# A decoder layer with routed experts: late groups closer together, two scatter sequences per step, two load queues in the tail, fewer idle products

## The reference

```python
x = x + attn(layernorm(x))                 # 16 heads of 8, rotary positions, softmax over 128 keys
x = x + cross_attn(layernorm(x), ctx_1024) # 16 heads of 8, softmax over 77 keys
x = x + ffn(layernorm(x))
# ffn: logits = x @ Wg + bg; top 2 of 8 experts, softmax over the two
#      y_e = gelu(x @ W1[e] + b1[e]) @ W2[e] + b2[e]   (128 -> 512 -> 128), the two chosen ones weighted
#      layernorm(x + y) * gamma + beta
```

## Time and profile before

| | |
|---|---|
| median of 3 runs | 647.62 us (645.97 to 648.56) |
| the profiled execution's own time | 647.97 us |
| its span, first to last instruction | 646.1 us |
| PE busy | 555.5 us, 86% of the span |
| DVE, ACT, POOL busy | 399.4, 336.5, 334.8 us (62%, 52%, 52%) |
| mean granted PE clock | 0.941 of full |

### The profile page before, as it was taken

How to read it: one execution, slowest core, us unless ns; L and a number is a source line. 1 busy time by engine, 2 the same in 40 slices (tenths; PEclk the granted TensorE clock), 3 DMA queues, 4 the chain that set the end, 5 groups by cost and what they waited for, 6 DMA issues and landing times.

```text
span 646.1 us, 22061 instructions
## 1 busy us (share of the span) xinstructions
PE 555.5 (86%) x7748; PEld 410.8 (64%) x7750; DVE 399.4 (62%) x1351; ACT 336.5 (52%) x869; POOL 334.8 (52%) x461
## 2 busy tenths in 40 slices
PE   4548899899999999999899997998877999999791
PEld 1224656556576666566666775677877999999530
DVE  3375778576677767758667564465666555555275
ACT  1113656466576566566666663354644455555243
POOL 4322735353353683773744655447646444444375
PEclk9687999899999999999999997598998899999996
DMA  3440323214158251060210331012213222221292
GB/s 104 140 138 9 89 73 100 67 55 138 31 183 250 65 168 60 15 196 31 77 51 31 111 88 43 14 44 72 80 54 93 67 70 66 54 58 55 68 261 82
DMA packets 74434, 55.73 MB, mean 86 GB/s; under 512 B 9024, under 2 KB 70981, under 8 KB 74338
## 3 DMA queue, kind: packets, MB, share of 16 engines
q1 hardware_dynamic: 69954, 45.92, 25.4%
q0 software_dynamic: 4384, 8.53, 4.0%
HBM read 33.62 MB, written 19.23 MB: 82 GB/s over the span
## 4 chain that ended last, share of the span: by engine, by line
PE 54%; DVE 20%; issue 9%; POOL 6%; ACT 3%; DMA 3%; SPq 2%; DVEq 2%; POOLq 0%; ACTq 0%
DVE nmp L1205 7%; PE AV L775 7%; PE S L949 7%; PE AV L874 5%; PE ST L743 5%; PE W L819 5%; PE SM L800 3%; PE AV L965 3%; PE SM L965 3%; PE ST L749 3%; PE S L711 2%; DVEq L1484 2%; DVE onorm L1216 1%; PE SM L788 1%; POOL routed L1665 1%
## 5 line engine op out<-in xcount | busy, mean ns | idle before, releaser
L1205 DVE TENSOR_REDUCE nmp<-S 128x4 bf16<-128x512 f32 (+1 forms) x256 | 142.2, 578 | 70.1 <-PE S L711 70.1
L1017 ACT ACTIVATE prob<-ST 128x512 f32<-128x512 f32 (+1 forms) x256 | 138.3, 591 | 73.0 <-PE ST L749 72.7
L1131 ACT ACTIVATE va<-S,b1s 128x128 f32<-128x128 f32 x288 | 82.2, 369 | 77.7 <-PE S L949 76.9
L1730 POOL DMA_INDIRECT expert_out<-va,ks x72 | 71.0, 986 | 72.2 <-DVE va L1511 62.9
L743 PE MATMUL ST<-nmt,onesr 32*77 32x128 bf16 (+1 forms) x1024 | 76.5, 224 | 15.8 <-DVE nmp L1205 12.2
L949 PE MATMUL S<-va 128*128 128x128 f32 x576 | 82.0, 287 | 8.8 <-DVE va L1499 8.6
L743 PEld LDWEIGHTS ST<-nmt,onesr 32*77 32x77 bf16 (+1 forms) x1024 | 55.3, 105 | 49.7 <-issue 45.0
L775 PE MATMUL AV<-prob,va 77*32 77x128 f32 (+1 forms) x2048 | 85.5, 286 | 0.0
L949 PEld LDWEIGHTS S<-va 128*128 128x128 f32 x576 | 73.1, 199 | 14.0 <-DVE va L1499 13.7
L1665 POOL DMA_INDIRECT routed<-pay,dest x64 | 66.0, 1031 | 17.8 <-issue 17.2
L874 PE MATMUL AV<-onesr,idb 128*128 128x256 bf16 x435 | 72.5, 285 | 0.0
(11 more groups left out here) (226 smaller groups left out, 1142.0 us busy)
## 6 DMA issues: line engine op xcount, KB each, us to landing
ks<-routed SPq DMA_DIRECT2D x72, 65.0 KB, 1.8
qs<-q_parts SPq DMA_DIRECT2D x32, 128.0 KB
ks<-k_parts SPq DMA_DIRECT2D x32, 128.0 KB, 2.7
q2s<-q_parts SPq DMA_DIRECT2D x32, 128.0 KB
k2s<-k_parts SPq DMA_DIRECT2D x32, 77.0 KB
xin<-x SPq DMA_DIRECT2D x8, 256.0 KB, 3.2
q_parts<-rpart SPq DMA_DIRECT2D x8, 256.0 KB
k_parts<-rpart SPq DMA_DIRECT2D x8, 256.0 KB, 3.4
```

Source lines behind the costliest of these rows:

```text
L1017: act.activation(prob[0:st.keys, j, :], ST[j % 2][0:st.keys, :], ACT.Exp, scale=SCALE).then_inc(s_exp, 1)
L1131: last = act.activation(ht[:, k, q, :], S[k][:, q * P:(q + 1) * P], ACT.Gelu, bias=b1s[:, bass.ds(b + q, 1)])
L1205: V.tensor_reduce(nmp[:, st.at % 2, row_tile(p), 0:NB], S[p % 2][:, 0:NB * st.keys].rearrange("p (b k) -> p b k", b=NB), AX.X, ALU.max, ne ...
L1730: pool.indirect_dma_start(out=expert_out, out_offset=bass.IndirectOffsetOnAxis(ap=xr[:, c % ROUND, D + 1:D + 2].bitcast(U32), axis=0), in_ ...
```

## The change

Five edits: `LATE` goes from 51 to 43, so that group 3 is late as well and POOL normalises at the end of a step from step 43; late groups scatter one sequence (two scatters) per step over four steps, instead of three scatters per step over three; `add_beta` moves from POOL to DVE for groups 3 and 4; in a step with projections the idle products ahead of `values(before, 1)` go away (`idle_at(st, 1)` is 0) and those ahead of `values(st, 0)` stay at 3; in the tail ACT issues two of the sixteen `y2` loads, PE runs 20 idle products ahead of the sums, POOL keeps the gamma product for chunks 1 and 3 alone, and chunk 7 is finished and stored in halves. With the scatters go semaphores for each sequence instead of one count, and two buffers of row numbers (`dest`).

```diff
-LATE = 51
+LATE = 43
...
+BETA = 3
...
-        if g < EARLY:
+        if g < BETA:
             job(last + 5, "beta", g)
...
-                    n = i * TOPK + k
-                    at, place = (chosen + 1 + n // 3, n % 3) if last >= LATE else (chosen + 1 + i, k)
-                    job(at, ("scatter", place), (g, i, k))
+                    job(chosen + 1 + i, ("scatter", k), (g, i, k))
...
-        def scat_count(g):
-
-            return 16 * (GS * TOPK * (g + 1) + 1)
+        def wait_scattered(eng, g, seqs=range(GS)):
+
+            for i in seqs:
+                eng.wait_ge(s_scat[g % 2][i], 16 * TOPK * (g // 2 + 1))
...
+        ON_POOL = (1, 3)
+        LAST = CHUNKS - 1
...
+        FIRST_Y2 = 2
...
-            sp.wait_ge(s_scat, scat_count(EARLY))
+            for g in (EARLY - 1, EARLY):
+                wait_scattered(sp, g)
             sp.wait_ge(s_tab, 1)
...
+                    if not (k and n < FIRST_Y2):
+                        load_y2(sp, n, k)
...
+            for n in range(LAST):
                 sp.wait_ge(s_fin, n + 1)
...
+                store(n * FC, FC)
+            sp.wait_ge(s_fin, LAST + 1)
+            store(LAST * FC, FC // 2)
+            sp.wait_ge(s_fin, LAST + 2)
+            store(LAST * FC + FC // 2, FC // 2)
...
-            def idle_at(st):
-
-                own = [name for j in range(NJ) for name, g in items_at(st, j)]
-                return 3 if st.slot < SEQS or any(name in PROJECTIONS for name in own) else 6
+            def idle_at(st, m):
+
+                own = sum(name in PROJECTIONS for j in range(NJ) for name, g in items_at(st, j))
+                if own == 0:
+                    return 3 if st.slot < SEQS else 6
+                return (3, 0)[m]
...
                 if before:
-                    dense(idle_at(st), AV[:, 2 * L:4 * L])
+                    dense(idle_at(st, 1), AV[:, 2 * L:4 * L])
...
             for n in range(4):
                 tokens_of(n)
+            pe.wait_ge(s_yw, NT)
+            dense(20, W[0][:, :])
...
             expert_turns(act, turn, between)
-
+            for k in range(4):
+                act.wait_ge(s_sc[k], 16 * NT // 4)
+            for n in range(FIRST_Y2):
+                load_y2(act, n, 1)
...
-                if i in (20, 22, 24):
-                    add_beta(EARLY + (i - 20) // 2)
+                if 20 <= i < 30 and i % 2 == 0:
+                    add_beta(BETA + (i - 20) // 2)
...
+            def chunk_out(n):
+                if n < LAST:
+                    part_out(n, n * FC, FC)
+                else:
+                    part_out(n, n * FC, FC // 2)
+                    part_out(n, n * FC + FC // 2, FC // 2)
```

More of the change, by code:

```diff
@@ L317, in decoder_layer @@
         destf = sb("destf", [P, GS, TOPK])
-        dest = sb("dest", [P, GS, TOPK], I32)
+        dest = sb("dest", [P, 2, GS, TOPK], I32)
         w1s = sb("w1s", [P, E * HID])
@@ L431, in decoder_layer @@
         s_hot = sem("s_hot")
-        s_scat = sem("s_scat")
+        s_scat = [[sem(f"s_scat{r}{i}") for i in range(GS)] for r in range(2)]
+        s_filler = sem("s_filler")
         s_out = sem("s_out")
@@ L669, in _ @@
             sp.wait_ge(s_fill, 16 * (E + 1))
-            sp.wait_ge(s_scat, scat_count(NG - 1))
+            for g in (NG - 2, NG - 1):
+                wait_scattered(sp, g)
             sp.wait_ge(s_tab, 2)
@@ L678, in _, with store @@
                 for k in range(TOPK):
-                    r0 = k * NTOK + n * FC * L
-                    sp.dma_start(y2[n][:, k, :].rearrange("p (s d) -> p s d", d=D),
-                                 expert_out[r0:r0 + FC * L, :].rearrange("(s p) d -> p s d", p=P)).then_inc(s_y2[k][n], 16)
-            for n in range(CHUNKS):
-                sp.wait_ge(s_fin, n + 1)
-                sp.dma_start(out_rows[:, n * FC:(n + 1) * FC, :],
-                             x2all[:, n * FC * D:(n + 1) * FC * D].rearrange("p (s d) -> p s d", d=D)).then_inc(s_out, 16)
-            sp.wait_ge(s_out, 16 * CHUNKS)
+                    if not (k and n < FIRST_Y2):
+                        load_y2(sp, n, k)
+            def store(first, seqs):
+                sp.dma_start(out_rows[:, first:first + seqs, :],
+                             x2all[:, first * D:(first + seqs) * D].rearrange("p (s d) -> p s d", d=D)).then_inc(s_out, 16)
+            for n in range(LAST):
+                sp.wait_ge(s_fin, n + 1)
+                store(n * FC, FC)
[3 more added lines that the diff above has]
+            store(LAST * FC + FC // 2, FC // 2)
+            sp.wait_ge(s_out, 16 * (CHUNKS + 1))
         @block.tensor
@@ L1316, in place @@
                 own = pay[:, g % 2, :, :, :]
+                if g >= 2:
+                    wait_scattered(dve, g - 2)
                 dve.wait_ge(s_gexp, g + 1)
@@ L1638, in norm_instance @@
                 else:
-                    if st.i == 0:
-                        g = st.group
-                        if g == 0:
-                            pool.wait_ge(s_none, 4)
-                        if g >= 2:
-                            pool.wait_ge(s_scat, scat_count(g - 2))
+                    g = st.group
+                    if st.at == CROSS_STEP[0]:
+                        pool.wait_ge(s_none, 4)
+                    if g >= 2:
+                        wait_scattered(pool, g - 2, (st.i,))
+                        if st.i == 0:
                             pool.wait_ge(s_keep[g % 2], 16 * (g // 2))
@@ L1699, in step @@
                     add_beta(g)
-                scatters(n, 2)
                 if n >= LATE:
@@ L1754, in _ @@
                     inverse_deviations(n)
-                if n and (n - 1) % 2:
+                if n - 1 in ON_POOL:
                     pool.wait_ge(s_norm, n * FC)
-                    times_gamma(G, n - 1)
+                    times_gamma(G, (n - 1) * FC, FC, s_gam[1])
 ARRAYS = ("x", "ctx_t", "w_self", "b_self", "bp", "w_cross", "b_cross", "bo", "wg", "bg", "w1", "b1", "w2", "b2",
```

45 lines of the change are left out of this document (25 added, 20 removed).

## The result

The changed kernel took **625.42 us** (median of 4 executions, 622.60 to 627.62), the kernel before, run beside it, 648.09 us (4 executions, 645.97 to 648.97). The ratio is 0.965, with a 95% interval of 0.960 to 0.971. Forecast were 623.6 us, in 615 to 635. The profiled execution took 627.59 us, with a span of 625.7.

The account below looks back on a forecast made before the run. PE was taken as the bound, with POOL's queue making one stall and half clock behind it. Terms of 13.3 + 9.2 + 0.4 - 0.4 + 1.9 = 24.4 us off 647.97 gave 623.6 us, range 615 to 635.

Parts of the forecast that it names:

- The stall and the half clock: Attention stage from step 54: PE's 3.5 us wait for POOL and 27 us at half clock vanish, 13.3 us gained.
- prediction's own tests the first: PE's clock: the prediction is wrong if it drops anywhere between step 10 and the first turn.
- the second fails at group 6: Test on PE's waits: the prediction is wrong if POOL is still the one that PE waits for.
- The idle products: Projection steps up to 53: three fewer idle products, 0.33 us at each of 29 groups; 9.2 us gained, bounds 4.8 to 9.6.
- the second rival: At `x3t` of group 6 or the first load: stall stays or returns, one half-clock stretch, 635 us; chance 0.15.
- Group 3 late: Around step 48: `choose` no longer precedes `norm_rows` on DVE; half of a 0.83 us wait saved, 0.4 us.
- Beta: Between turns: two more additions on DVE cost 0.4 us, bounds nothing to 1.4 us.
- The tail: Final sums and stores: 0.6 us lost at the first sum, 2.1 and 0.4 gained at the end; 1.9 us gained.
- The sign of under 4.5 us: Tail: the next profile would show under 4.5 us from L1553's counterpart to the last addition.
- The slower rival: Projection steps: fewer products let the clock fall, 11 us per 27 us stretch, 657 us with three; chance 0.06, 0.04 slower.

Follow-up runs that it names:

- POOL's order alone: Changed kernel with the idle products and tail of the kernel before, against the kernel before: 637.7 us, ratio 0.983.
- tail of before: Changed kernel with the kernel before's tail (one load queue, no 20 idle products, last chunk whole), against the kernel before: 626.6 us, ratio 0.966.
- without the 20: Changed kernel without the 20 idle products of 512 columns ahead of the final sums, against the kernel before: 625.2 us, ratio 0.965.
- sets 1 and 2: Two groups of follow-up kernels, each run on one chip beside the kernel before, which took 650.3 and 649.6 us there.
- three scatters: Changed kernel with late groups' scatters again three, three and two to a step, against the kernel before: 633.7 us, ratio 0.977.
- k2 earlier: Changed kernel with the k2 projection of group 7 one step earlier, against the kernel before: 622.6 us, ratio 0.960.
- set 3: Third group of follow-up kernels, run on one chip beside the kernel before, which took 700.7 us there.

## Why the prediction was right, point by point

- **The stall and the half clock: 13.3 forecast, 13.5 measured.** The mechanism is the one forecast; POOL's order alone shows it. In the changed kernel SP's first load comes 21.86 us earlier, step 54 8.35 us: 13.5. That this agrees to 0.2 us is in part luck, for two misses cancel: counted from step 54, `x3t` of group 6 comes 13.9 us earlier and not 15.3, since the wait for `k2s` stands ahead of it, and the first load loses 0.4 us behind it and not 2.0. SP waited for the scatter there, as forecast: its first load comes 3.5 us behind the start of the last scatter. But that starts 6.2 us behind `x3t` of group 6 where 7.2 were taken, and so the load comes only 1.4 us behind the table (1.1 before). Of the prediction's own tests the first holds from step 11 to the first turn, where the clock is full; a stretch of half clock at 113 to 120 us lies in steps 9 and 10. By the letter the second fails at group 6, where PE still waits 0.83 us for POOL.
- **The idle products: 9.2 forecast.** Each projection step is 0.33 us shorter, but for steps 26 and 34 (0.08) and step 29 (0.8). Steps 1 to 8 and 11 to 53 of the changed kernel with the tail of before are 10.3 us shorter than with POOL's order alone, so the term was 1 us small. Steps 9 and 10 took 1.9 us back in the changed kernel's trace (a wait of 2.85 us for `ks` from `k_parts`, 1.86 before, and 6.8 us at half clock instead of 3.4). The kernel without the 20 has the same 6.8 us there; six other traces of sets 1 and 2 with the idle edit have no half clock in these steps. **What the step missed** is the k2s wait of step 57. I looked for what PE meets later among DVE's waits and not among SP's transfers. It costs 1.3 us and, in some executions, a stretch of half clock: the second rival, with another cause than it named. PE's being faster explains only part of it. The transfer that parks `k2` in `k_parts` and the product that needs `k2s`, before and after:

```profile
380.38 0.37 SPq L559 DMA_DIRECT2D k_parts<-k2part  x1
388.89 0.25 PE L743 MATMUL ST<-nmt,onesr 32*77 32x128 bf16 x2
...
371.85 0.37 SPq L572 DMA_DIRECT2D k_parts<-k2part  x1
```

Before, 8.5 us pass between them without a wait. After, PE is there 8.2 us behind the parking and starts at 381.34, 9.5 us behind it. So PE comes 0.3 us earlier, and the transfers are ready at least 1.0 us later, counted from the parking; in the six other traces with this wait they take 9.1 to 10.3 us. Why they take longer is open.
- **Group 3 late: 0.4 forecast, 0.6 measured**: with POOL's order alone, steps 46 to 50 take 25.65 us instead of 26.22 (step 46 longer by 1.2; 47, 48 and 50 shorter).
- **Beta: -0.4 forecast.** The expert stage lost 1.1 us. That beta is its cause is not borne out: three other kernels with the addition on DVE (POOL's order alone, tail of before, without the 20) took 169.5 to 170.2 us, less than the 170.7 before, so 1.1 us is within what traces differ by. Up to the next load behind the fillers SP's queue carries the time (it starts 63.3 us after the first load before and 63.4 after), and what PE gains between turns ends in the longer wait (4.50 us, 2.69 before). What the last 1.0 us went into is open.
- **The tail: +1.9 forecast, -0.4 measured. This is the term that failed**, in three of its pieces. At the first sum I took 1.0 us of delay by the 20 products and nothing by the second queue: it is 1.2 us, and by the queue, behind which the first load lands 1.2 us later (4.09 us instead of 2.93), while the products end within that wait. What the products give back, full clock behind a wait of over 3 us, I did not count, since the trace of before had it anyway. At the end, L1582 takes 0.17 us as forecast, and gamma and residual of a half chunk 0.43 and 0.42 us where I took 0.36: from L1582 to the last addition pass 5.5 us instead of 7.2, so -1.7 of -2.1. (The sign of under 4.5 us did not follow from the sum, which gives 5.1.) What was not in the sum at all is the end of the path. I followed DVE's last addition and the store, but before and after the span ends with POOL's closing piece; SP was through 2.5 us behind the last addition before and 2.0 after, so the store did get shorter and never counted. POOL's last instruction comes 2.4 us earlier (+31.6 instead of +34.0), and the closing piece, by the split semaphores, is 2.8 us longer: together the 0.4 us lost.
- **The slower rival** (the clock falls in projection steps): not seen between steps 11 and 53 of the changed kernel. Of the eight traces of sets 1 and 2 and the result that have the idle edit, two have one stretch of half clock of 3.4 us there: three scatters in step 41 (1.5 us longer) and k2 earlier in step 24 (0.8 us longer); the two without the edit have none. So the rival may be at work at a small price, which no run here settles. Half clock beside the wait for `k2s` is the larger risk.

In all, 24.4 us were forecast and 22.7 came between the medians (20.4 between the profiled spans). The executions of the changed kernel come in two kinds, 623 and 627.6 us (granted clock 0.96 and 0.95), and the profiled one is of the longer kind.

## What to carry to other kernels

When work is taken from the engine that leads, list the transfers whose start it sets and whose end it waits for: they do not get faster with it (here they took longer), and the first of them to be late is the next stall. Two edits that each take time from the same clock-bound stretch are to be run apart and together; here one alone could cost most of its own gain. A block of transfers on an in-order queue costs what stands behind it, and spreading it among the loads was worth about a third of the whole change (5.9 to 6.5 us between the first load and the last scatter, 8 to 9 us in the medians). And the end of a program has a price of its own: read what lies between each engine's last instruction and the end of the span.

## What the hardware showed unexpected

- Half clock held for 64.8 us with PE busy 63.2 of 64.7 us: a busy PE is no guarantee that the clock returns soon. It held for 20 to 27 us in four other stretches of the traces outside set 3.
- A wait of 1.21 us was followed by half clock, one of 1.30 us in nearly the same code was not.
- POOL's closing piece takes 4.5 us with one semaphore for its scatters and the filler, 7.3 with nine, 7.1 with five. It is no fixed price for each; what it does hang on stays open.
- A second queue for the loads of the tail made the first of them later: it landed 3.8 to 4.3 us behind its issue in five traces, and 2.9 to 3.1 us in the five with one queue.
- The kernel before took 648 to 650 us in the first result and in sets 1 and 2, and 700.7 us in set 3; the traces of that set have waits from step 28 on whose cause is open.
